# Both halves of a chunk's value product in one visit of TensorE, in the causal batches of an attention and mixture-of-experts kernel

## The reference, cut to what matters

```python
def _L1_attn_ref(x, w_in, b_in, w_out, b_out):
    qkv = x @ w_in.T + b_in
    q, k, v = jnp.split(qkv, 3, axis=-1)
    ...
    scores = jnp.einsum('bhqd,bhkd->bhqk', q * scale, k)
    scores = scores + causal_bias
    attn = jax.nn.softmax(scores, axis=-1)
    out = jnp.einsum('bhqk,bhkd->bhqd', attn, v)
    ...
```

```python
    x = x + 0.5 * _L0_ffn_ref(_layernorm(x, axis=-1), ...)
    x = x + _L0_attn_ref(_layernorm(x, axis=-1), ...)
    x = x + 0.5 * _L0_ffn_ref(_layernorm(x, axis=-1), ...)
    x = x + 0.5 * _L1_ffn_ref(_layernorm(x, axis=-1), ...)
    x = x + _L1_attn_ref(_layernorm(x, axis=-1), ...)
    x = x + 0.5 * _L1_ffn_ref(_layernorm(x, axis=-1), ...)
```

## Time and profile before

| | |
|---|---|
| median of 3 runs | 998.64 us (998.04 to 999.71) |
| span of the profiled execution | 996.2 us |
| TensorE, VectorE, ScalarE busy | 89%, 76%, 68% of the span |
| mean granted TensorE clock | 0.974 |
| first causal group of batches | about 316 to 467 us |
| second causal group of batches | about 791 to 963 us |

### The profile page before, as it was taken

One profiled execution on the slowest core, in us unless ns is written; L12 is line 12 of the kernel. 1 busy time (PEld: TensorE's weight loads), 2 busy tenths in 40 slices (PEclk: granted clock), 3 DMA queues, 4 the chain that ended last, 5 costly groups with the idle time before them and its releaser, 6 DMA issues.

```text
span 996.2 us, 25709 instructions
## 1 busy us (share of the span) xinstructions
PE 890.2 (89%) x10020; PEld 474.5 (48%) x10020; DVE 759.1 (76%) x1352; ACT 674.5 (68%) x1470; POOL 331.3 (33%) x603
## 2 busy tenths in 40 slices
PE   2699999898888899999999998889798989999998
PEld 1123333235877455554323333249685545555565
DVE  5889999873536887888999999916347888888646
ACT  2388887687666677777798877786462367777631
POOL 4454312241655323332232412416651132311101
PEclk9699999999989999999999999999899999999999
DMA  4117740010133211111111100010310222110000
GB/s 145 51 35 189 189 108 13 16 34 22 39 112 107 63 51 43 46 51 40 34 45 31 44 18 2 24 42 31 98 57 1 64 66 57 43 38 5 3 22 22
DMA packets 60521, 52.32 MB, mean 53 GB/s; under 512 B 9106, under 2 KB 57362, under 8 KB 60402
## 3 DMA queue, kind: packets, MB, share of 16 engines
q1 hardware_dynamic: 48980, 40.00, 14.9%
q10 hardware_dynamic: 8478, 4.62, 2.1%
q0 software_dynamic: 2944, 6.05, 1.9%
HBM read 13.64 MB, written 11.06 MB: 25 GB/s over the span
## 4 chain that ended last, share of the span: by engine, by line
PE 57%; DVE 20%; ACT 10%; issue 7%; POOL 3%; DMA 2%; ACTq 1%; DVEq 0%; POOLq 0%; SPq 0%
PE ps L594 14%; PE ps L675 14%; DVE negm L957 10%; ACT pt L795 8%; PE ps L740 5%; PE ps L724 4%; PE ps L733 4%; DVE blockm L948 3%; PE ps L600 3%; PE ps L630 3%; PE ps L746 2%; PE ps L683 2%; PE ps L693 2%; PE ps L635 2%; DVE l_stats L992 1%
## 5 line engine op out<-in xcount | busy, mean ns | idle before, releaser
L795 ACT ACTIVATE pt<-ps 128x512 f32<-128x512 f32 (+1 forms) x896 | 458.2, 566 | 151.6 <-PE ps L594 101.5
L957 DVE TENSOR_REDUCE negm<-ps 128x2 f32<-128x1024 f32 x256 | 300.7, 1219 | 27.5 <-PE ps L594 25.5
L675 PE MATMUL ps<-pt,va 128*32 128x256 f32 (+1 forms) x4352 | 273.9, 340 | 11.8 <-ACT ot L801 5.0
L948 DVE TENSOR_REDUCE blockm<-ps 128x8 f32<-128x1024 f32 (+1 forms) x192 | 194.6, 1042 | 31.4 <-PE ps L594 20.1
L594 PE MATMUL ps<-ks,qs 61*128 61x128 bf16 (+2 forms) x1536 | 172.6, 291 | 31.4 <-DVE negm L957 17.3
L594 PE MATMUL ps<-qs,ks 64*128 64x128 bf16 (+3 forms) x1408 | 167.9, 295 | 6.1 <-ACT pt L795 2.0
L675 PEld LDWEIGHTS ps<-pt,va 128*32 128x32 f32 x4352 | 91.9, 108 | 125.0 <-issue 80.8
L594 PEld LDWEIGHTS ps<-ks,qs 61*128 61x128 bf16 x1536 | 54.5, 95 | 184.4 <-issue 85.6
L1225 POOL CAST mpart<-negm 128x16 bf16<-128x16 f32 x64 | 13.3, 209 | 296.3 <-DVE negm L957 153.6
L829 ACT ACTIVATE stage<-ps,pt 128x128 f32<-128x128 f32 x240 | 68.7, 371 | 30.5 <-PE ps L724 29.5
L594 PEld LDWEIGHTS ps<-qs,ks 64*128 64x128 bf16 x1408 | 57.9, 94 | 59.7 <-ACT pt L795 45.1
(11 more groups left out here) (150 smaller groups left out, 1062.7 us busy)
## 6 DMA issues: line engine op xcount, KB each, us to landing
qs<-parts SPq DMA_DIRECT2D x80, 128.0 KB
ks<-parts SPq DMA_DIRECT2D x77, 128.0 KB
experts<-in_experts SPq DMA_DIRECT2D x8, 578.0 KB, 5.5
sorted<-stage ACTq DMA_DIRECT2D x4, 967.5 KB, 8.4
qs<-mrow SPq DMA_DIRECT2D x128, 6.0 KB
pt<-y_rows SPq DMA_DIRECT2D x8, 256.0 KB, 3.1
qs<-parts SPq DMA_DIRECT2D x32, 56.0 KB
ks<-parts SPq DMA_DIRECT2D x30, 56.0 KB
```

The costliest lines, as they stand in the source:

```text
L675: ins = pe.matmul(pv_bank[32 * j:32 * j + 32, q0:q1], va[n % 2][:, kb, value_at(g, j):value_at(g, j) + 32], pt[:, k_, from_:from_ + q1 - q ...
L795: a.activation(pt[:, k_ % NPT, S * s:S * s + width], b_bank(o + s)[:, 0:width], ACT.Exp).then_inc(b_free, 1)
L948: v.tensor_reduce(blockm[:, g % 2, :, t, PLACES[c_]], pair_of(ka)[:, :, 0:width].rearrange("p s (b c) -> p s b c", c=P), AX, ALU.max, nega ...
L957: v.tensor_reduce(negm[:, g % 2, :, t, c_], pair_of(ka), AX, ALU.max, negate=True).then_inc(a_free, 1)
```

## The change

`V_LATER`, the number of slots from the second step of a chunk to half 0 of its values (half 1 came one later), becomes a table: (2, 3) for non-causal batches, as before, and (3, 3) for causal ones. The offsets of the events behind the values are written as numbers that give the same slots.

```diff
-V_LATER = 2
+V_LATER = {False: (2, 3), True: (3, 3)}
...
                 for half in range(2):
-                    due.append((slot + V_LATER + half, "pv", n, (g, i // 2, half)))
+                    due.append((slot + V_LATER[causal_of[n]][half], "pv", n, (g, i // 2, half)))
                 if i == nstep[Q] - 1 and g % 2:
-                    due.append((slot + V_LATER + 1, "evac", n, g // 2))
-                    due.append((slot + V_LATER + 3, "o", n, g // 2))
+                    due.append((slot + 3, "evac", n, g // 2))
+                    due.append((slot + 5, "o", n, g // 2))
                     if g == 3:
-                        due.append((slot + V_LATER + 5, "onT", n, None))
-                        due.append((slot + V_LATER + 7, "out", n, None))
+                        due.append((slot + 7, "onT", n, None))
+                        due.append((slot + 9, "out", n, None))
```

## The result

The changed kernel takes **1015.29 us** (median of 4 runs, 1013.52 to 1016.86) where the kernel before takes 999.17 us (4 runs, 998.04 to 1000.17): a ratio of 1.0162, 95% interval 1.0148 to 1.0177. That is 16.1 us more; the forecast was 11.9 more. One execution of the kernel of experiment 7 took 1336.57 us at a mean granted clock of 0.555, and is left out of that kernel's numbers.

What follows compares the result with a forecast made beforehand. The chain showed TensorE leading, with ScalarE ending a tenth of the path. Batch terms 2.8 + 3.8 + 1.5 + 3.2 + 0.6 = 11.9 us, added to 998.64, gave 1010.6 us; range 1002 to 1018.

Steps and rivals of the forecast that it cites:

- the three waits per round: Causal rounds: score steps wait for exponentials about 0.3, 0.7 and 0.5 us in every round.
- The quiet round: Shortest of a causal batch's four rounds, without projections or transposes: walked from 7.70 to 7.93 us, 0.23 more.
- The second half pays no entry: Joined value visits: no entry assumed for the second half; the rival had a full 0.15 us each, 1025 us, chance 4 in 100.
- The switches do not decide: Rival for causal score and value visits: saved switches decide, 24 us go, 974.6 us; chance 7 in 100.
- Nothing evened out: Rival: chunk 1's wait is hidden in most rounds, savings and waits cancel, 997 to 1000.6 us; chance 8 in 100.
- an exponential of 512 columns takes 0.54 us: ScalarE in the quiet round: one 512-column exponential takes 0.54 us, two take 1.09.
- the walk of the old order: Check on the quiet round before the change: the same walk gives every start within 0.03 us.
- batch 15: 1.1 - 0.5: Last causal batch: two full rounds cost 1.1 us; its last two, covered by feed-forward work, save 0.5.
- 4 and 12: 1.4 each: First batch of each causal group, without an earlier batch's transposes and bound by reductions: 1.4 us more each.
- rival 4: The granted clock falls: each of 32 rounds loses 1 us, 1043 us; chance 1 in 100.
- 13 and 14: 1.6 each: Second causal group: 1.6 us more each, some new waiting falling where VectorE already held TensorE.
- batch 7: Last batch of the first causal group, sharing two rounds with the next batch's longer reductions: 1.5 us more.

Runs made afterwards that it cites:

- experiment 7: Kernel before, with exponentials cut to 32 columns and row maxima to 32 of each 128 in batches 5 to 7 and 13 to 15: 983.87 us.
- experiments 7 and 8: Exponentials and row maxima both shortened in batches 5 to 7 and 13 to 15: kernel before 983.87 us, changed kernel 983.45 us.
- experiment 11: Changed kernel, with the first round of batches 4 and 12 left in the old order: 1014.33 us.
- experiment 12: Changed kernel, with only chunk 2's halves joined and m one slot earlier in causal batches: 1002.79 us.
- experiments 4, 9 and 11: Changed kernel with both halves one step earlier, 1010.98 us; kernel before with m one slot later in causal batches, 1017.0 us; and experiment 11.

## Why the prediction was right, and where its sizes were off

**Right in sign, mechanism and range.** The forecast was 1010.6 us (1002 to 1018; its own terms give 1010.54), measured are 1015.29. ScalarE's share of the chain is 22.7% ("near 20%" was said), the value pair takes 1.01 us, the non-causal stretch kept its length, the three waits per round are there. The quiet round was walked as 7.93 and took 8.08; each start of the walk is within 0.15 us. The batch is 39.06 us, walked 38.62.

**Rivals.** The second half pays no entry: 1.01 and 0.58 us for the visits are the sizes walked without one. The switches do not decide while exponentials and reductions have their length; experiments 7 and 8 show them deciding in the steady batches once both are cut. Nothing evened out. The clock is the one that I judged too lightly (below).

**Step "an exponential of 512 columns takes 0.54 us".** I halved the 1.09 of a pair. The p2 of 361.52 needs the first of the pair that began at 360.86 and came 0.66 us after it, where the walk had 0.59; with the same 0.05 behind it the first ends after 0.61 and the second after 1.08. The trace of before had it too: in the quiet round the exponentials begin at 359.12, and the p2 that needs the first of them stands 0.65 behind,

```profile
359.77 0.39 PE L594 MATMUL ps<-qs,ks 64*128 64x384 bf16 x4
```

and the earlier trace rows has 0.60 for a single instruction of ScalarE over 128x512, the evacuation. That start isn't among, so the walk of the old order, 0.06 early there, seemed exact. About the same 0.06 stands in chunk 2. Through the two such waits a round the walk of the batch was short: 2.32 instead of 1.88 per full batch. In batches 5 and 6 this is 0.9 us of the table. That the 0.06 makes up the whole 0.44 is shown only in the quiet round; for the other three I have the totals (0.78, 0.49, 0.67 against 0.73, 0.39, 0.53).

**Term "batch 15: 1.1 - 0.5".** Here the sign was wrong. I had its last two rounds saving entries because feed-forward work would cover. Their score steps have no p1 in between, and behind a first p2 TensorE waits by up to 0.69 us (PE of the changed kernel):

```profile
969.77 0.39 PE L594 MATMUL ps<-qs,ks 64*128 64x384 bf16 x4 [0.69 <-ACT pt L795]
```

From o to o there it is 22.38 us where it was 21.03, +1.35 instead of a saving. With fewer instructions around, the value visit was a larger part of the cover, not a smaller one.

**Terms "4 and 12: 1.4 each".** Less the 0.73 of the next batch's round that lies in the same stretches, they cost 3.1 and 2.1 us. Batch 4's first round went from 10.01 to 11.86 us, and in it a joined visit of 32 matmuls took its modelled 1.94 us instead of 1.08 at the low clock:

```profile
334.75 1.94 PE L675 MATMUL ps<-pt,va 128*32 128x128 f32 x32
```

So a low clock for longer, and slower matmuls: rival 4 in small, at two or three places instead of all 32 rounds. That the new waits bring it isn't shown. The kernel with chunk 2 alone joined has the old order in this whole round and yet a granted clock of 0.79 from 332 to 336 us, where the kernel before has 1.00, and its first stretch is only 0.33 us longer than before. Batch 13's excess (2.65 against 1.6) is the clock's: the slice of 0.62 from 880 to 884 us costs 1.47 (experiment 11), and without it the batch pays 1.18. Of the 18.8 us this 1.47 is the clock's for certain, and the visit of 334.75 adds 0.86; how much more of the group starts is the clock stays open.

**Term "13 and 14: 1.6 each".** Batch 14's 1.54 is as forecast; batch 13's would be 1.18, below it, at the full clock.

The table's stretches exceed the forecast by 6.9 us. The first exponential's 0.06 and batch 15 are 2.6 of these (0.9 and 1.7), the group starts 2.4, batch 13 1.05, and batch 7 0.9, of which some 0.4 would be the exponential's again and the rest is open. By the medians the excess is 4.2: 2.7 us belong to which executions were profiled.

## What to carry to other kernels

Before joining two visits of an in-order engine, ask what waits the separate visits cover: walk one round by starts, with the buffers that each score step needs, and price the gap that opens against the switch that goes. Join only where something else already stands in the gap; here that was chunk 2, whose visit stood between the two longest score steps (a p1 of 0.45 us is left in the gap), and finding it took one run per chunk. And count every engine that the visit hides: with ScalarE's waits shortened, VectorE's were next.

## What the hardware showed that was not expected

- Two exponentials of 128x512 back to back take 1.08 us, but a reader of the first one's bank got it about 0.61 us after the start (0.66 by starts, less 0.05), not 0.54. Halving a group's time gives a first element too early.
- A saved switch is worth 0.22 us where nothing waits (2.69 against 2.47 us in chunk 0 of experiments 7 and 8), near the 0.25 for entering and leaving that the earlier trace rows show. Over the batch only 0.07 a visit is left of it (12 visits, 0.88 us): where other work stands between the steps only the entering is saved, and ten waits of 0.17 us are left in the 80 us from 372 to 452.
- From m's transpose to the p2 that reads it were 4.27 us, by a copy on ScalarE and two DMAs of 1.56 us together at issue; the kernel before gives it 4.57 us (m at 360.26, that p2 at 364.83), so a slack of only 0.3 to 0.5 us hid it, an estimate (from the issue of the DMAs to that p2 it is 2.91 against 3.37 us).
- The granted clock can fall in the middle of a causal group (0.62 from 880 to 884 us in the changed kernel, 0.64 from 912 to 916 us with chunk 0 alone joined, 0.58 from 904 to 908 us in experiment 12 behind its 1.92 us of waiting). The kernel before has no such slice there. Not every kernel that waits more has one: those of experiments 4, 9 and 11 don't, the last with the same waits as the changed kernel ahead of that place.
